# Bf16 copies of the slot networks' weights made during the first attention stage, and a last pass whose input is fetched during the slot update

## The reference, cut to what matters

```python
h = gelu(concat(x, mean(S)) @ w1 + b1);  logits = (h @ w2 + b2) / (abs(tau) + 0.1)
alpha = softmax over the top 8 of 64 slots
si = einsum('ts,td->sd', alpha, x) / alpha.sum(0)             # needs all 4096 tokens
gi = si @ Wih.T + bih;  gh = S @ Whh.T + bhh                  # GRU step on 64 slots
S_new = gru(gi, gh, S)
q, k, v = S_new @ wq, S_new @ wk, S_new @ wv;  y = layernorm(S_new + attention(q, k, v))
slot_values = y @ wvp + bvp
out = einsum('ts,sd->td', alpha, slot_values) @ wo + bo        # again all tokens
```

## Time and profile before

| what | us |
|---|---|
| runs of before | 2418.47, 2419.16, 2472.72; median 2419.16 |
| the profiled execution's own time | 2417.27 |
| its span on the slowest core (core 6) | 2415.7 |
| other cores' spans | 2402.4 to 2415.2 |
| attention A, to its barrier | about 0 to 647 |
| f1 with its slot update | 647 to 903 |
| attention B | 903 to 2097 |
| f2: token blocks | 2097 to 2266 |
| f2: slot update | 2266 to 2323 |
| f2: last pass | 2323 to 2415.7 |

### The profile page before, as it was taken

One profiled execution on the slowest core, in us unless ns is written; L12 is line 12 of the kernel. 1 busy time (PEld: TensorE's weight loads), 2 busy tenths in 40 slices (PEclk: granted clock), 3 DMA queues, 4 the chain that ended last, 5 costly groups with the idle time before them and its releaser, 6 DMA issues.

```text
span 2415.7 us, 43084 instructions; the slowest of 8 cores (2402.4 to 2415.7 us)
## 1 busy us (share of the span) xinstructions
PE 1770.4 (73%) x14656; PEld 995.9 (41%) x14810; DVE 1473.1 (61%) x2438; ACT 1022.7 (42%) x1560; POOL 843.9 (35%) x709
## 2 busy tenths in 40 slices
PE   4979999898556753577888878877888787567653
PEld 2434444444333321344554545544555555233310
DVE  4355747553265544677777777777777766367443
ACT  0057575757243411244445444444445454245200
POOL 1000000000121102367666666667666676311000
PEclk9989999998779875689999999999999999789765
DMA  9313323122499974301222111211221200399559
GB/s 205 60 36 99 112 80 119 67 71 88 108 218 212 207 123 108 122 19 45 71 71 71 62 57 50 71 62 53 71 71 62 71 27 27 106 226 225 129 159 328
DMA packets 92726, 251.72 MB, mean 104 GB/s; under 512 B 13249, under 2 KB 21569, under 8 KB 92516
## 3 DMA queue, kind: packets, MB, share of 16 engines
q1 hardware_dynamic: 52020, 179.06, 22.8%
q0 software_dynamic: 35888, 53.13, 14.9%
q10 hardware_dynamic: 4608, 16.78, 1.9%
HBM read 234.17 MB, written 67.90 MB: 125 GB/s over the span
## 4 chain that ended last, share of the span: by engine, by line
PE 50%; DVE 18%; issue 10%; DMA 8%; ACT 8%; POOL 4%; DVEq 1%; SPq 0%; ACTq 0%; POOLq 0%
PE bF L1794 9%; PE aF L412 6%; PE bF L1908 5%; PE aF L430 4%; ACT Wslot L487 3%; PE aO L445 3%; PE aS L464 3%; PE bF L1732 2%; PE bF L1804 2%; DMA out<-xout 2%; PE f_F L896 2%; PE bF L1780 2%; DVE b_Pb L2223 2%; ACT hfeat L2011 1%; DVE b_khf L2202 1%
## 5 line engine op out<-in xcount | busy, mean ns | idle before, releaser
L487 ACT ACTIVATE Wslot<-aS,cvals_s 128x1024 bf16<-128x1024 f32 (+3 forms) x384 | 327.2, 900 | 174.8 <-PE aS L464 174.0
L1697 POOL TENSOR_TENSOR xout<-b_m,b_hf 128x1024 bf16<-128x1024 bf16 x128 | 269.6, 2123 | 150.6 <-DVE b_m L2167 110.2
L1794 PE MATMUL bF<-xout,Wslot 128*128 128x256 bf16 x2048 | 252.2, 283 | 23.5 <-DVE xin L2136 10.0
L1794 PEld LDWEIGHTS bF<-xout,Wslot 128*128 128x128 bf16 x2048 | 202.2, 101 | 74.2 <-issue 43.0
L618 POOL TENSOR_SCALAR ave<-amv 128x1 f32<-128x1 f32 x32 | 8.3, 260 | 455.1 <-DVE amv L500 455.1
L2167 DVE TENSOR_TENSOR b_m<-bB,b_xx 128x1024 bf16<-128x1024 f32 x128 | 155.5, 1216 | 12.9 <-POOL xout L1697 8.8
L464 PE MATMUL aS<-aQf,aKf 64*128 64x512 bf16 (+3 forms) x768 | 131.9, 339 | 26.6 <-ACT Wslot L487 20.1
L445 PE MATMUL aO<-aVaug,Wslot 128*128 128x65 bf16 x2304 | 129.3, 198 | 25.3 <-DVE Wslot L552 24.8
L1908 PE MATMUL bF<-Wslot,b_ygT 128*128 128x512 bf16 x481 | 119.0, 390 | 16.4 <-DVE htok L2255 15.0
L445 PEld LDWEIGHTS aO<-aVaug,Wslot 128*128 128x128 bf16 x2304 | 91.1, 100 | 81.2 <-issue 69.5
L2011 ACT ACTIVATE hfeat<-bF 128x512 bf16<-128x512 f32 x128 | 76.0, 594 | 96.9 <-PE bF L1794 96.3
(11 more groups left out here) (302 smaller groups left out, 3857.3 us busy)
## 6 DMA issues: line engine op xcount, KB each, us to landing
xin<-x1d SPq DMA_DIRECT2D x64, 512.0 KB, 8.4
xin<-x3d SPq DMA_DIRECT2D x48, 512.0 KB, 9.1
xin<-x SPq DMA_DIRECT2D x32, 512.0 KB, 4.6
xout<-x SPq DMA_DIRECT2D x32, 512.0 KB, 4.4
x1d<-xout SPq DMA_DIRECT2D x32, 512.0 KB, 2.9
x2d<-xin SPq DMA_DIRECT2D x32, 512.0 KB, 5.5
xin<-x2d SPq DMA_DIRECT2D x32, 512.0 KB, 4.1
x3d<-xin SPq DMA_DIRECT2D x32, 512.0 KB, 3.0
```

The costliest lines, as they stand in the source:

```text
L487: e_ex.inc(a.activation(Pk[:, :, qo:512], psS[i % 2][:, :, 0:512 - qo], AF.Exp, bias=cvals[:, 1:2], scale=0.125), s)
L1697: return eng.tensor_tensor(dst, mm[:].rearrange("p (a o q) -> p a o q", a=2, o=2), hf[n % 2][:, 2 * s:2 * s + 2, :].unsqueeze(1).broadcast_to(
L1794: mm = t.matmul(ps[:, o * 256:(o + 1) * 256], w[:, dc, oc * 128:(oc + 1) * 128], mixb[:, sl, dc, :], start=(dc == 0), stop=(dc == NDC - 1))
```

## The change

It has three parts.

- Twelve new DRAM tensors `half[...]` hold bf16 copies of weights of f1, f2 and three of attention B. pool() of attention A issues one copy, DRAM to DRAM and float32 to bf16, before the layer-norm step of each of the tiles 4 to 15, and waits for the last at the end of the stage. The later loads read the copies.
- In f2, all tiles of the last pass but two have buffers of their own, made of eight `xt` tiles and the weight buffers that mid has finished with. Their loads are issued in groups during mid, each after the product that used the buffers last. Tiles 30 and 31 reuse the buffers of tiles 0 and 1 after these are stored. VectorE waits for a group instead of a tile.
- The constant `onesf` (128x144) is replaced by a 1x128 tile that f1 loads. This frees 576 bytes per partition, and one load less stands at the kernel's start.

```diff
+    half = {nm: nc.dram_tensor(nm + "_h", list(sh[nm].shape), BF16,
+                               kind="Internal").ap()
+            for nm in ("fw1b", "fw1a", "fWhhT", "fwv", "fwvp", "fwo", "fwq", "fwk",
+                       "fWihT", "bWk", "bWr", "bWo")}
...
+            copies = iter(half)
             for g in range(32):
+                if g >= 4:
+
+                    for nm in itertools.islice(copies, 1):
+                        e_half.inc(gp.dma_start(out=half[nm][:, :],
+                                                in_=dram[nm][:, :]), nm)
                 e_mv.wait_ge(gp, g)
...
+            e_half.wait_ge(gp, "bWo")
...
-                e_0["w1b"].inc(gp.dma_start(out=w1b, in_=rows(dram["fw1b"])), 0)
-            e_w["1"].inc(gp.dma_start(out=w1a, in_=rows(dram["fw1a"])), 0)
+                e_0["w1b"].inc(gp.dma_start(out=w1b, in_=rows(half["fw1b"])), 0)
+            e_w["1"].inc(gp.dma_start(out=w1a, in_=rows(half["fw1a"])), 0)
...
+            groups = [range(0, 4), range(4, 8), range(8, 12), range(12, 16),
+                      range(16, 20), range(20, 22), range(22, 26),
+                      range(26, 30), range(30, 31), range(31, 32)]
+            e_y = [ev(f"y{i}", g, 16) for i, g in enumerate(groups)]
...
+            xs = (xt + f4[0] + f4[1] + f4[2]
+                  + [w0[:, 4096 + 2048 * i:6144 + 2048 * i].bitcast(F32)
+                     for i in range(2)] + f4[3] + f4[4] + xt[0:2])
...
-                e_y[g % 8].wait_ge(v, g)
+                e_y[grp[g]].wait_ge(v, groups[grp[g]][-1])
...
+            d_["LN"].wait_ge(s_, ("LN", 31))
+            ldy(groups[0])
+            ldy(groups[1])
+            for k in range(2):
+                mp.wait_ge(s_, ("gi", 2 * k + 1))
+                ldy(groups[2 + k])
+            mp.wait_ge(s_, ("gi", 5))
+            ldln()
+            ldy(groups[4])
+            mp.wait_ge(s_, "k")
+            ldy(groups[5])
+            mp.wait_ge(s_, "v1")
+            ldy(groups[6])
+            mp.wait_ge(s_, "sv")
+            ldy(groups[7])
+            for g in (30, 31):
+                e_s01[g - 30].wait_ge(s_, g - 30)
+                ldy(groups[g - 22])
+            e_st.wait_ge(s_, 31)
```

More of the change, by code:

```diff
@@ L1 @@
 import contextlib
+import itertools
 import numpy as np
@@ L255, in build @@
     onesb = sb("onesb_s", (128, 72), BF16)
-    onesf = sb("onesf_s", (128, 144), F32)
     cvals = sb("cvals_s", (128, 8), F32)
@@ L270, in f @@
                              (maskB, "maskB"),
-                             (onesb, "onesb"), (onesf, "onesf"),
+                             (onesb, "onesb"),
                              (cvals, "cvals")):
@@ L363, in emit_attn_a @@
         e_mv = Ev(ctx, "dve_LS", range(32))
+        e_half = Ev(ctx, "half", half, 16)
         e_ve = Ev(ctx, "ve", range(32))
@@ L715, in emit_ffn @@
             tau = fsb("tau", (1, 4), F32)
+            onesf = fsb("onesf", (1, 128), F32)
             hst = [aT[:, 2048 + i * 1024:3072 + i * 1024].bitcast(F32)
@@ L789, in emit_ffn @@
         if not first:
-            e_y = [ev(f"y{i}", range(i, 32, 8), 16) for i in range(8)]
-            e_st = [ev(f"st{i}", range(i, 32, 8), 16) for i in range(8)]
+            groups = [range(0, 4), range(4, 8), range(8, 12), range(12, 16),
+                      range(16, 20), range(20, 22), range(22, 26),
+                      range(26, 30), range(30, 31), range(31, 32)]
+            e_y = [ev(f"y{i}", g, 16) for i, g in enumerate(groups)]
+            grp = {t: i for i, g in enumerate(groups) for t in g}
+            fl = [w[:].rearrange("p a b -> p (a b)") for w in (*W[1:4], wv_, wvp_)]
+            f4 = [[w[:, 2048 * i:2048 * (i + 1)].bitcast(F32) for i in range(4)]
+                  for w in fl]
+            xs = (xt + f4[0] + f4[1] + f4[2]
+                  + [w0[:, 4096 + 2048 * i:6144 + 2048 * i].bitcast(F32)
+                     for i in range(2)] + f4[3] + f4[4] + xt[0:2])
+            e_s01 = [ev(f"s2_{i}", [i], 16) for i in range(2)]
+            e_st = ev("st0", range(2, 32), 16)
         wparts = {"1": 2, "qk": 2, "v": 1, "vp": 1, "o": 1}
@@ L843, in pe @@
                 pre_v.wait_ge(t, "tau")
-                pre_p.inc(t.matmul(psL[:, 0:1], onesf[0:1, 0:128], tau[0:1, 2:3],
+                pre_p.inc(t.matmul(psL[:, 0:1], onesf[:], tau[0:1, 2:3],
                                    start=True, stop=True), "sm")
@@ L1073, in act @@
                 p2v.wait_ge(a, (g, 1))
-                e_st[g % 8].inc(a.dma_start(out=x_out[g * 128:(g + 1) * 128, :],
-                                            in_=xt[g % 8]), g)
+                ins = a.dma_start(out=x_out[g * 128:(g + 1) * 128, :], in_=xs[g])
+                (e_s01[g] if g < 2 else e_st).inc(ins, g)
         def dve(v):
@@ L1269, in dve @@
                     p2p.wait_ge(v, (g, h))
-                    x = xt[g % 8][:, h * 512:(h + 1) * 512]
+                    x = xs[g][:, h * 512:(h + 1) * 512]
                     p2v.inc(v.tensor_tensor(x, ps[:, 0:512], x, ALU.add), (g, h))
@@ L1289, in pool @@
                         out=Wih[i][:],
[L1290 to L1293, removed]
+                        in_=rows(half["fWhhT"][:, i * 1024:(i + 1) * 1024])), 0)
+            e_w["v"].inc(gp.dma_start(out=wv_[:], in_=rows(half["fwv"])), 0)
+            e_w["vp"].inc(gp.dma_start(out=wvp_[:], in_=rows(half["fwvp"])), 0)
+            e_w["o"].inc(gp.dma_start(out=wo_[:], in_=rows(half["fwo"])), 0)
             if not first:
@@ L1297, in pool @@
                         out=Wih[i][:],
-                        in_=rows(dram["fWihT"][:, i * 1024:(i + 1) * 1024])), 0)
+                        in_=rows(half["fWihT"][:, i * 1024:(i + 1) * 1024])), 0)
             if first:
                 pre_p.wait_ge(gp, "b1")
-            e_w["qk"].inc(gp.dma_start(out=wqk[:, :, 0:256], in_=rows(dram["fwq"])), 0)
-            e_w["qk"].inc(gp.dma_start(out=wqk[:, :, 256:512], in_=rows(dram["fwk"])), 1)
+            e_w["qk"].inc(gp.dma_start(out=wqk[:, :, 0:256], in_=rows(half["fwq"])), 0)
+            e_w["qk"].inc(gp.dma_start(out=wqk[:, :, 256:512], in_=rows(half["fwk"])), 1)
             for tok in order:
@@ L1324, in pool @@
                     bw_pre[key].inc(gp.dma_start(
-                        out=W[j][:], in_=rows(dram["bW" + key])), 0)
+                        out=W[j][:], in_=rows(half["bW" + key])), 0)
             mvv.wait_ge(gp, "mv")
@@ L1343, in sp @@
                 e_0["b"].inc(s_.dma_start(out=tau[0:1, 0:1], in_=dram["ftau"][:, :]), 2)
-                e_0["b"].inc(s_.dma_start(out=bst[0:1, 0, 0, 0:1],
-                                          in_=dram["ftau"][:, :]), 3)
+                e_0["b"].inc(s_.dma_start(out=onesf[:], in_=dram["onesf"][0:1, 0:128]),
+                             3)
             for g in range(4):
@@ L1382, in sp, with ldy, ldln @@
             e_w["ca"].inc(s_.dma_start(out=S0f, in_=dram["fslot"][:, :]), 4)
[L1384 to L1398, removed]
+            def ldy(gs):
+                for g in gs:
+                    e_y[grp[g]].inc(s_.dma_start(
+                        out=xs[g], in_=x_in[g * 128:(g + 1) * 128, :]), g)
+            def ldln():
+                mvv.wait_ge(s_, "Sn")
+                for i, (dst, src) in enumerate(((lng, "flngc"), (lnb, "flnbc"))):
+                    e_w["ln"].inc(s_.dma_start(out=dst, in_=dram[src][:, :]), i)
             if first:
+                ldln()
                 return
[L1401 to L1404, removed]
+            d_["LN"].wait_ge(s_, ("LN", 31))
[5 more added lines that the diff above has]
+            mp.wait_ge(s_, ("gi", 5))
+            ldln()
+            ldy(groups[4])
[9 more added lines that the diff above has]
+            e_st.wait_ge(s_, 31)
         blk.tensor(pe)
```

## The result

| | before | changed |
|---|---|---|
| median, us | 2418.81 | 2488.01 |
| ratio to before | 1 | 1.029, 95% interval 1.0267 to 1.0314 |
| span of the profiled execution, slowest core | 2415.7 | 2485.6 |

What follows compares the result with a forecast made beforehand. Stages were bound differently: the last pass by moving 29.4 MB, f1 by uncovered transfers and otherwise VectorE's pace. Terms -38 - 6 - 8 - 3 + 2 = -53 gave 2366 us, range 2350 to 2400 (first case 2347 to 2385).

Steps and rivals of the forecast that it cites:

- term 5: Attention A: weight copies fit in free DMA time, residual tiles just covered; 0 to 8 us lost, 2 taken.
- Term 1: Last pass: 22 of 24 loads taken out, stores end last; gain 38 us, bounds 30 to 45.
- The slot update at nothing: f2's slot update: prefetching 22 more tiles costs nothing, ldln landing with a margin of 12 us.
- Term 2: Start of f1: w1b's lighter packets load faster; gain 6 us, bounds 0 to 8.
- Term 3: f1, round trips of H: lighter weights ahead in queue 0 cut VectorE's waits; gain 8 us, bounds 2 to 13.
- Term 4: Start of f2: the fifth input tile comes sooner beside lighter weights; gain 3 us, bounds 1 to 5.
- rival of too slow a copy: End of attention A: the wait for bWo delays the stage if copies run too slowly; 2699 us at 60 GB/s, chance 0.06.
- The rate: Attention A: copies read at 312 GB/s, 181 us of DMA time for 56.6 MB read.
- attention A gives it back: Attention A: late residual tiles or reciprocal deviations lose 32 to 48 us; 2398 to 2414 us, chance 0.12.
- The slower rival: End of attention A: copies below 93 GB/s decide, the wait for bWo lengthening the stage; 2699 us at 60 GB/s, chance 0.06.
- slower by over 2%: Whole kernel: time more than 2% (48 us) above before; chance 0.05.

Runs made afterwards that it cites:

- e4: Changed kernel without copies, all weights loaded as float32, keeping the last-pass prefetch and small constant: 2381.18 us, ratio 0.983 to before.
- e5: Changed kernel with copies in small pieces (4 KB read), one instruction per token tile from 4 on, the sixteenth (bWo) at tile 30: 2383.5 us, ratio 0.984 to before.
- e7: Kernel before with small-piece copies spread one per token tile and bf16 loads, keeping the last pass of before: ratio 1.001 to before.
- e6: Changed kernel with small-piece copies at its own places but without the last copy, bWo loaded as float32: 2379.97 us in one run.
- e1: Changed kernel with each copy cut into pieces of one row, at most 4 KB read, at the same places: 2492.15 us, ratio 1.029 to before.
- e11: Changed kernel with small-piece copies spread one per token tile, the sixteenth at tile 19 (about 290 us): 2461.12 us in one run.
- e8: Changed kernel with small-piece copies of fw1b, fw1a and fWhhT alone, other weights loaded as float32: 2378.6 us, ratio 0.983 to before.
- e9: Changed kernel with large-packet copies of fw1b, fw1a and fWhhT alone, other weights loaded as float32: 2372.56 us in one run.
- e2: Changed kernel with copies in pieces of 16 KB read (12 KB for the two wide tensors): 2462.95 us in one run.

## Why the prediction was wrong, step by step

Forecast were 2366 us, 53 less than before; measured were 2488, 69 more. Nearly all of the difference is term 5.

- **Term 1** (-38, measured -37): right in mechanism and size, by the changed kernel, e4, and e5 against e7 (55.1 and 92.8). Stores took 46.2 us where I had 45.4.
- **The slot update at nothing:** right to within 1 us or so. With the prefetch it is 54.4 to 55.7 in the experiments against 54.5; the 56.5 of the changed kernel is not explained.
- **Term 2** (-6): w1b won 6.7 us, in 11.97 us where 11 to 15 were forecast.
- **Term 3** (-8): too large; f1 won 10.6 in all, which leaves 3.9, and the six blocks only 2.2 (124.2 us where 110 to 118 were forecast). A row cost 101 ns, and the weights up to wo had landed 84 us after f1's first load, both near the low ends of 85 to 136 and 81 to 109. But H came 78 us after it, and the sum had left out wq and wk, which stand behind wo in queue 0 and landed at 853.7. H's first round trip landed at 853.1: it stayed 10.95 us, where under 6 was forecast, and only the later ones fell. New packets of 2 KB alone, the thing that was priced, did not occur: two rows were joined in each.
- **Term 4** (-3, measured +1, and 0 to +1 in e5, e6 and e7, which have the same weights in f2): wrong, small. VectorE's wait for input tiles in f2 fell from 10.4 to 7.0 us, and the stage did not get shorter.
- **Term 5** (+2, measured +118): the failed step. I wrote that a residual tile "would take 10 instead of 4.5 us as in f1", and in the rivals that "the copies share the engines packet by packet with queue 1". The second sentence is true and defeats the first. The price of sharing by packets is the size of the other's packet, and I took f1's (4 KB read) for a copy that is contiguous on both sides, whose packets are 64 KB. A transfer took 33 to 42 us instead of 10 where it went at its own pace, they piled up in SyncE's queue, and the awaited residual tile took 140.4. I had "unknown division into packets" in my text, but only beneath the rival of too slow a copy.
- **The rate** of 312 GB/s of reads was too high as well: 216 to 222. That the writes now go to the same memory is a likely reason, but no run shows it. The first five copies ended at 199 and not at 165, the last at 363 and not by 350, still long before the stage.
- **The rivals:** the one that came was "attention A gives it back", with 0.12, by its own mechanism (late residual tiles). Its price, 32 to 48 us, was made of 16 small waits and not of the one large. The slower rival (a copy below 93 GB/s) named another place and did not come. No rival reached 2488 by what happened, and "slower by over 2%" had only 0.05.

That the reciprocal deviations on GpSimd could be held up by its own DMA issues, I had costed at 0.91 us each. With large packets that is right (0.6 to 1.1 us each); e1 and e11 show that it turns into 86 to 128 us with many small pieces.

## What to carry to other kernels

A transfer that is put into idle DMA time is not hidden by the idle time alone: price each foreground transfer as its own packets, and those of the transfers queued before it, times the background's packet time, until the background ends; and look at how the background's access pattern is cut, since one that is contiguous on both sides gets the largest packets. Cutting it small has a price too, in the engine that issues it, so place copies where no tile is awaited. And measure which of the copies pays: here two of twelve gave half of what f1 could win, and the fetch of the last pass, which needed none of them, gave nearly all of the gain in the total.

## What the runs showed of the hardware

- A DRAM to DRAM copy with contiguous sides was cut into packets of 65.5 KB read and 32.8 KB written, 4.7 us each (changed kernel, 240 to 260); by rows of 4 KB it ran at the same rate of about 108 GB/s written (e8, e9).
- Two queues that both had work got equal numbers of packets in 20 us: 65 and 63 with large ones (changed kernel), 363 and 365 with 16 KB ones (e2).
- Loads without a cast joined two rows of 2 KB into one packet of 4 KB, 202 ns each (changed kernel, 790 to 830); with the cast a row was a packet, 207 ns (before).
- GpSimd stood for 86 and 128 us before its twentieth transfer of 1024 pieces in attention A, until all earlier ones had landed (e11, e1); with the queue empty it did not (e5).
